# Graph layer on one NeuronCore: empty places of the gathered bins get an index beyond the table

## The reference

```python
xn = _layernorm(x, axis=-1)
x = x + segment_sum(edge_weight[:, None] * xn[dst], src, 6250) + mix(xn)
x = x + moe(_layernorm(x, axis=-1))      # 8 experts, top 2 of them
```

## Time and profile before

| | |
|---|---|
| Median of three runs | 2460.81 us (2460.7 to 2463.82) |
| The profiled execution, its own time | 2458.35 us |
| Its span | 2456.3 us |
| Mean granted TensorE clock | 0.923 |
| Busy: PE, DVE, POOL, ACT | 2061.3, 1568.4, 1458.9, 1088.6 us |

### The profile page before, as it was taken

One profiled execution on the slowest core, in us unless ns is written; L12 is line 12 of the kernel. 1 busy time (PEld: TensorE's weight loads), 2 busy tenths in 40 slices (PEclk: granted clock), 3 DMA queues, 4 the chain that ended last, 5 costly groups with the idle time before them and its releaser, 6 DMA issues. The chain is left out here.

```text
span 2456.3 us, 42316 instructions
## 1 busy us (share of the span) xinstructions
PE 2061.3 (84%) x11854; PEld 1780.8 (72%) x11854; DVE 1568.4 (64%) x2897; ACT 1088.6 (44%) x3196; POOL 1458.9 (59%) x1280
## 2 busy tenths in 40 slices
PE   6884268999999999989998999899999784888840
PEld 3673257888888788878887888788888684667630
DVE  6446988866886697578758875886444458222225
ACT  3421025555555555555555555555666420222210
POOL 0001037877877787688768777887777430777740
PEclk9997689999999999999999999999999857999975
DMA  7216012223222323232332223222333420666657
GB/s 240 86 43 214 9 38 80 85 84 96 82 84 85 96 76 88 83 94 80 89 92 84 86 83 94 82 85 84 91 102 101 127 79 1 197 198 199 203 165 239
DMA packets 145273, 259.49 MB, mean 106 GB/s; under 512 B 26627, under 2 KB 97266, under 8 KB 144915
## 3 DMA queue, kind: packets, MB, share of 16 engines
q0 software_dynamic: 59584, 161.78, 22.2%
q1 hardware_dynamic: 70734, 75.75, 10.1%
q10 hardware_dynamic: 14724, 19.20, 2.2%
HBM read 211.84 MB, written 39.36 MB: 102 GB/s over the span
## 5 line engine op out<-in xcount | busy, mean ns | idle before, releaser
L766 POOL DMA_INDIRECT edge_G<-xn_scratch,edge_row_i x1029 | 1206.8, 1173 | 393.8 <-issue 269.5
L883 ACT ACTIVATE edge_weighted<-edge_hots,edge_scale 128x128 f32<-128x128 bf16 x2401 | 738.6, 391 | 31.6 <-DVE edge_row_hots L1072 16.3
L839 PE MATMUL edge_op<-edge_win,edge_A 128*128 (+1 forms) x2744 | 654.0, 382 | 0.0
L839 PEld LDWEIGHTS edge_op<-edge_win,edge_A 128*128 128x128 f32 x2744 | 527.1, 192 | 72.5
L834 PE MATMUL edge_op<-edge_G,edge_weighted 128*128 128x256 f32 x2058 | 513.7, 387 | 41.6 <-DVE all_xn L1082 33.9
L875 ACT COPY edge_A<-edge_ap 128x512 f32<-128x512 f32 x343 | 200.8, 585 | 646.2 <-PE edge_ap L825 646.2
L1067 DVE TENSOR_TENSOR edge_hots<-edge_iota128b,edge_recb 128x1024 bf16<-128x1024 bf16 x343 | 237.4, 692 | 306.4 <-PE edge_ap L825 272.7
L834 PEld LDWEIGHTS edge_op<-edge_G,edge_weighted 128*128 128x128 f32 x2058 | 370.5, 194 | 84.2 <-issue 46.9
L825 PE MATMUL edge_ap<-edge_weighted,edge_row_hots 128*128 128x128 f32 x2744 | 371.0, 279 | 21.9 <-ACT edge_weighted L883 21.5
L825 PEld LDWEIGHTS edge_ap<-edge_weighted,edge_row_hots 128*128 128x128 f32 x2744 | 340.0, 193 | 52.6 <-issue 43.1
L812 PE MATMUL edge_bp<-edge_RH,edge_SL 128*128 128x245 bf16 x1568 | 213.2, 282 | 43.9 <-DVE edge_SL L1033 43.9
(11 more groups left out here) (244 smaller groups left out, 1884.7 us busy)
## 6 DMA issues: line engine op xcount, KB each, us to landing
exp_w1x<-in_w SPq DMA_DIRECT2D x105, 256.0 KB
edge_G<-xn_scratch,edge_row_i POOLq DMA_INDIRECT x1029, 3.0
comb_ys<-ys_scratch SPq DMA_DIRECT2D x12, 1024.0 KB, 7.1
ln_xin<-in_x SPq DMA_DIRECT2D x12, 512.0 KB, 5.2
xn_scratch<-ln_xnb ACTq DMA_DIRECT2D x12, 512.0 KB, 5.6
all_xn<-ln_xnb ACTq DMA_DIRECT2D x12, 512.0 KB, 6.3
mix_xin<-in_x SPq DMA_DIRECT2D x12, 512.0 KB, 3.8
sum_scratch<-all_xn SPq DMA_DIRECT2D x1, 6144.0 KB
```

Source lines behind the costliest of these rows:

```text
L766: pool.indirect_dma_start(out=G[:, row_buffer(b), i, :], out_offset=None, in_=xn_dram, in_offset=bass.IndirectOffsetOnAxis(ap=row_i[:, b * ...
L839: last = nc.tensor.matmul(op[j][:, :], A[:, j, i, :], w, start=False, stop=i == DN - 1)
L883: last = nc.scalar.activation(weighted[:, buf, i, :], hots[:, b % 2, i // 2, :, i % 2], ACT.Copy, scale=scale[:, b, i:i + 1])
```

## The change

A gathered place without an edge gets the index 12544 + `low` - 1 in place of `low`, which is beyond the last row, 6249; the gather gets a bound, and leaves such a row of its buffer as it is. So that an empty place can be told from a relative row of 0, `low` of the gathered chunks is lowered by one, and relative rows begin at 1. `G` is set to zero once at the start of the stage, so that a row that was never written holds a number.

```diff
+        vacant = part[:, 0:GN, :].rearrange("p k b -> p (k b)").rearrange("p (b k) -> p b k", k=GN)
...
-        LINKS = 1 + LP + 2 + 2 + 1 + CB + 1
+        LINKS = 1 + LP + 2 + 2 + 1 + CB + 4
...
             def _(pool):
+                nc.gpsimd.memset(G[:, :, :, :], 0.0).then_inc(rows_set, 1)
                 pool.wait_ge(e_in, 48)
...
                 pool.sem_inc(stepped, BEFORE)
+                pool.wait_ge(rows_set, 1)
...
-                                                                    axis=0)).then_inc(gathered[row_buffer(b)], 16)
+                                                                    axis=0),
+                                bounds_check=N - 1, oob_is_err=False).then_inc(gathered[row_buffer(b)], 16)
...
                 lows = lowb[:, :].rearrange("p (q k) -> p q k", q=NQ)
+                link(nc.vector.tensor_single_scalar(lows[:, :, 0:GN], lows[:, :, 0:GN], 1.0, op=ALU.subtract))
...
-                        nc.vector.tensor_tensor(next_rows[:, :, :], raw[:, 0:GN, 1, :].rearrange("p k b -> p b k"),
-                                                lows.to_broadcast([P, NB, GN]), ALU.add).then_inc(rows_ready, 1)
+                        places = raw[:, 0:GN, 1, :].rearrange("p k b -> p b k")
+                        next_link(q, nc.vector.tensor_scalar(vacant[:, :, :], places, 0.0, float(2 * NT * P),
+                                                             ALU.is_equal, ALU.mult))
+                        next_link(q, nc.vector.tensor_tensor(vacant[:, :, :], vacant[:, :, :],
+                                                             lows.to_broadcast([P, NB, GN]), ALU.add))
+                        next_link(q, nc.vector.tensor_tensor(next_rows[:, :, :], places, vacant[:, :, :], ALU.add))
+                        dve.sem_inc(rows_ready, 1)
```

More of the change, by code:

```diff
@@ L660, in edge_stage @@
         rows_taken = st.sem("rows_taken")
+        rows_set = st.sem("rows_set")
         low_ready = st.sem("low_ready")
```

## The result

The changed kernel takes 2509.35 us in the median (2504.65 to 2512.37), the kernel before in the same comparison 2462.32 us. The ratio is 1.0181, 95% interval 1.0149 to 1.0213: slower by 47 us between the medians. The forecast was 2463.0 us, at most 2471. The profiled execution took 2504.65 us, its span is 2502.6 us (46.3 more than before), the mean granted clock 0.92 as before.

A forecast was written before the change was run, and what follows sets the result against it. DVE was taken to bound the edge stage's prologue and TensorE the rounds, with gathers hidden almost everywhere. The terms +0.8 + 0.2 + 1.5 + 0.3 - 0.6 = +2.2 us on 2460.8 gave 2463.0 us, range 2459 to 2471.

The forecast's parts named there:

- The bound also adds a MOVE ... and I price it at nothing.: POOL's queue: a 29 ns MOVE, 1029 times, stands in no one's way because the queue runs ahead; cost nothing.
- So the bound costs from nothing to 46 + 25 = 71 ns ... I take 46 ns.: Each gather on POOL: the bound lengthens it by nothing to 71 ns, taken as 46 from the nearest pair.
- the second rival: The gather becomes the bound from about 55 ns more each; at 71 ns +9 us, about 2470; chance 0.17.
- In the last round 3 x 0.046 = 0.14 us go into 0.16 us of room, so nothing.: Last round, each step: three longer gathers still fit within TensorE's 3.91 us, so no loss.
- the rival's formula: Last round: loss starts where 3 x 1.25 + 3 x 0.055 passes 3.91 us; at 71 ns 2.4 us.
- three signs: Second rival's signs: unheld gathers over 1.02 us, last-round steps over 3.95 us, TensorE's waits for gathers over 15 us.
- That swallows small delays.: Rounds with binning: a gather held up by DVE ends about 0.95 us after DVE's instruction, however much earlier it began.
- Rows skipped: Gathers' transfers: 29% of rows, 39.5 of 134.9 MB, left out with packets unchanged; 0.13 us earlier arrival, 0.6 us off.
- the 0.6 us priced: Steps 4 and 13: gain taken for earlier arrival of rows, from a range of 0 to 1.5 us.
- DVE's work for the indices: Prologue: three linked instructions replace one, +0.8 us, and a subtraction on lowb, +0.2; nothing in the other six rounds.
- steps 4 and 13: Places without room for later gathers: +1.5 us at step 4 over five rounds, +0.3 at step 13 over six.
- The range: Whole kernel: 2459 to 2471 us, leaving out the faster case and the worst of the slower one.

The follow-up runs named there:

- e3_queue_only: The kernel before with one semaphore increment in POOL's queue ahead of each gather, no bound: 2656.52 us, ratio 1.002.
- e10_pool_longer: The kernel before with a one-column memset on POOL ahead of the three gathers of each step, no bound: 2477.92 us, ratio 1.0072.
- e13_bound_shared_fast: The changed kernel with its bound in a register loaded once ahead of the loop, at the first chip's speed: 2491.41 us, ratio 1.0119.
- e2_index_only: The changed kernel without the bound and with every index kept in the table; DVE's added work and the memset stay: 2643.23 us, ratio 0.9966.
- e15: The kernel before with one POOL memset of 200 columns ahead of the third gather of step 15: ratio 1.0004.
- e17: The kernel before with one POOL memset of 768 columns ahead of the third gather of step 15: ratio 1.0004.
- e11: The changed kernel with every gathered row skipped, so messages of the three gathered chunks are left out: 2487.65 us, ratio 1.0111.
- e14: The kernel before with only a bound loaded once ahead of the loop, nothing skipped, at the first chip's speed: 2494.93 us, ratio 1.0155.
- e4: The changed kernel with its bound in a register loaded once ahead of the loop, on a slower chip: 2679.27 us, ratio 1.011.
- e5: The kernel before with only a bound loaded once ahead of the loop, nothing skipped, on a slower chip: 2653.72 us, ratio 1.0026.

## Why the prediction was wrong

- **"The bound also adds a MOVE ... and I price it at nothing."** This step failed worst: 20 of the 46 us. I looked at the 29 ns and at who stands behind them, and they do cost nothing by themselves (e3_queue_only). What the MOVE does is to lengthen the loop's pass from 257 recorded instructions to 404, and behind each branch back the queue is silent for 2.3 to 2.6 us more. Shown by e10_pool_longer and e3_queue_only (silence without a bound) and by e13_bound_shared_fast (bound without the silence): 18 us with e10, and 1.0181 against 1.0119, 15 us, with e13.
- **"So the bound costs from nothing to 46 + 25 = 71 ns ... I take 46 ns."** It costs 54 ns, 947 to 1001. The bounds held, the value was 8 ns low, and it fell on the edge that the second rival names (55 ns).
- **"In the last round 3 x 0.046 = 0.14 us go into 0.16 us of room, so nothing."** Measured +6.2 us where the rival's formula gives nothing for 54 ns. The formula counts free gathers only. Once POOL's period exceeds TensorE's, its gathers drift against DVE's instructions, and from the 23rd step of the round on the third gather of nearly every step is held 0.05 to 0.3 us, which no longer goes into a pause. The second rival was right in kind here, and by its own sum (+9 in all) much too small. Two of its three signs came, steps of 4.09 us (over 3.95) and waits for gathers of 27.8 us (over 15); its gathers of over 1.02 us did not.
- **"That swallows small delays."** True at step 13, whose steps kept their length. It failed at steps 14 and 15: the small delay of three longer gathers puts the third one of step 15 where DVE pauses no more, and it is held for 2.5 us: +16.6. That it comes with the bound at this place is shown: at steps 15 and 16 each of the nine profiles with a bound has one to six gathers of over 3.4 us, and none of the eleven without. How the bound brings it about is not. e2_index_only has such a gather at step 12 without a bound, so it may be lateness alone, but e15 to e17, which were to show that, stopped 0.04 us short. Also, a held gather ends 0.8 to 0.9 us behind the DVE instruction, a little less than the 0.95 read: the row of line 1015 in the earlier trace rows is two instructions, and the first ends at 873.26.
- **Rows skipped: right.** 122.5 MB and 59,584 packets, as forecast; the median from issue to landing fell from 3.0 to 2.7 us, more than the 0.13 I gave. What it is worth in time isn't settled, but the 0.6 us priced are too little once POOL is the bound: e11 says some 17 us from 29% to 100% skipped. For the 29% themselves e13 against e14 says 9 us gained by the ratios and 4 by the medians, with intervals that touch; e4 against e5 says 22 us lost, at the other speed and on two chips.
- **DVE's work for the indices: right.** In DVE's timeline of after, in the prologue, three instructions take the place of one:

```profile
315.81 0.32 DVE L1051 TENSOR_SCALAR edge_part<-edge_raw 128x147 f32<-128x147 f32 x1
316.16 0.31 DVE L1053 TENSOR_TENSOR edge_part<-edge_part,edge_lowb 128x147 f32<-128x147 f32 x1
316.51 0.32 DVE L1055 TENSOR_TENSOR edge_next_rows<-edge_raw,edge_part 128x147 int32<-128x147 f32 x1
316.98 1.68 DVE L1031 TENSOR_REDUCE edge_slot<-edge_BH 128x30 bf16<-128x1470 bf16 x1
```

1.17 us to the next instruction in place of 0.24, so +0.93, and +0.21 for the subtraction, against +0.8 and +0.2. At step 28 nothing was lost (steps 16 to 47: 0.0), and e2_index_only agrees.
- **The sizes of steps 4 and 13** (+1.5 and +0.3) were not what moved: steps 1 to 13 came out at -0.7.
- **The range.** Its upper end came from the price of a longer gather alone. Neither an instruction's effect on the loop as a whole nor a hold-up that grows was in any case.

## What to carry to other kernels

An instruction added inside a long unrolled loop is also length of the loop: compare the instruction queue's packets and the time between the branch back and the next instruction before and after, and keep constants in registers loaded outside. A gather with a bound takes POOL no less for the rows that it skips; where the engine that makes descriptors has 0.05 us of room, 54 ns turn it into the bound. If such an engine runs with little room, try one more buffer: here it took 6 to 8 us off the kernel before and some 27 off the changed one.

## What the runs showed of the hardware that was not expected

- A pass of 257 recorded instructions on POOL's queue starts again 0.2 us after its branch; passes of 308 and 404 after 2.4 to 2.8 us, each with 5 more packets of 8 KB on the instruction queue.
- By the Trainium skill, "Advanced Engine Details and Errata", ISA Cache, the cache holds two lines of 256 instructions. That a longer pass restarts later agrees in kind; that moving the loop by 100 places changed nothing does not agree with the reading that counts lines from the start of the stream.
- A bound adds 54 ns to a gather on POOL (947 to 1001 ns) whether rows are skipped or not: none (1000), 29% (1001) or all of them (1000), in ns.
- Skipped rows keep their packets: 59,584 with 161.78, 122.48 and 27.44 MB.
- Two gathers that start within 10 ns of each other relative to DVE's work can take 1.08 or 3.55 us.
